# Between the states of a recurrence: pieces moved ahead of the last multiplications, experts' products weighted on ScalarE and added on GpSimd

## What is computed

```python
def _mamba_forward(x, W_in, conv_w, conv_b, W_xproj, W_dt, b_dt, A_log, D, W_out):
    u, z = jnp.split(x @ W_in.T, 2, axis=-1)
    uc = silu(conv3(u) + conv_b)            # depthwise, three taps over the sequence
    B_ssm, C_ssm, dt = split(uc @ W_xproj.T)
    delta = softplus(dt @ W_dt.T + b_dt)
    def step(h, inp):                       # over the 1024 positions, n = 16 states
        dA = jnp.exp(d_t[:, :, None] * A)
        h = dA * h + (d_t * u_t)[:, :, None] * b_t[:, None, :]
        y_t = jnp.einsum('bdn,bn->bd', h, c_t)
    return ((y + uc * D) * silu(z)) @ W_out.T

def _L0_ffn_ref(x, gate_w, W1, b1, W2, b2, sW1, sb1, sW2, sb2):
    combine = top-2 softmax weights, renormalised      # (tokens, 8)
    h = jax.nn.gelu(jnp.einsum('th,ehf->tef', x, W1) + b1)
    y = jnp.einsum('tef,efh->teh', h, W2) + b2
    return jnp.einsum('teh,te->th', y, combine) + gelu(x @ sW1 + sb1) @ sW2 + sb2
```

## Time and profile before

| | |
|---|---|
| median of 3 runs | 3067.3 us (3067.11 to 3069.73) |
| the profiled execution | 3073.01 us, of which the span of its instructions 3070.9 us |
| busy over the span | PE 78%, DVE 72%, ACT 55%, POOL 47% |
| loop of batch 0 | 72.8 to 270.6 us (197.8 us) |
| loop of batch 1, with the experts of batch 0 | 270.6 to 514.0 us (243.4 us) |
| loop of batch 2, with the experts of batch 1 | 514.0 to 766.7 us (252.7 us) |
| loop of batch 3, with the experts of batch 2 | 766.7 to 991.2 us (224.5 us) |
| experts of batch 3 | up products from 1031.3 us, last down product done 1158.4 us |
| the layers behind | the rest, to 3070.9 us |

### The profile page before, as it was taken

The page is one execution under the profiler, slowest core; times in us unless marked ns, Lnnn a source line. Parts: engine busy times, 40 slices in busy tenths (PEclk is TensorE's granted clock), DMA queues, the critical chain, the costliest instruction groups (busy, mean ns, idle before and its releaser), DMA issues.

```text
span 3070.9 us, 42340 instructions
## 1 busy us (share of the span) xinstructions
PE 2391.0 (78%) x15570; PEld 1711.5 (56%) x15570; DVE 2202.3 (72%) x3693; ACT 1696.2 (55%) x2621; POOL 1448.7 (47%) x1343
## 2 busy tenths in 40 slices
PE   2333579388488794999999999999999478767987
PEld 0101256156256572777677777777777356745675
DVE  5999999989986314888788878887888543354334
ACT  5333476376474342878777877787777224222322
POOL 0434323433433102655866676667567541564156
PEclk7555699698798896999999999999999789887988
DMA  3000000000000001101000000000000100000000
GB/s 103 0 0 0 1 1 1 0 1 1 0 1 1 1 1 40 26 24 29 21 23 22 22 22 22 22 22 21 22 22 1 42 1 1 1 14 1 1 1 14
DMA packets 32031, 42.04 MB, mean 14 GB/s; under 512 B 8897, under 2 KB 18130, under 8 KB 31442
## 3 DMA queue, kind: packets, MB, share of 16 engines
q1 hardware_dynamic: 31826, 39.34, 4.7%
HBM read 12.05 MB, written 2.10 MB: 5 GB/s over the span
## 4 chain that ended last, share of the span: by engine, by line
PE 49%; DVE 24%; issue 12%; POOL 9%; ACT 5%; SPq 1%; DMA 0%; POOLq 0%; DVEq 0%; ACTq 0%
PE ps L1073 10%; PE ps L1051 6%; PE ps L1062 6%; PE ps L828 5%; DVE MA L1209 3%; DVE lnb L315 2%; DVE BIG L340 2%; PE ps L757 2%; PE ps L1842 2%; PE ps L1033 2%; PE ps L759 2%; PE ps L758 2%; DVE BIG L334 2%; PE ps L1784 1%; DVE ps L328 1%
## 5 line engine op out<-in xcount | busy, mean ns | idle before, releaser
L1209 DVE TENSOR_REDUCE MA<-ps 128x1 f32<-128x1024 f32 x512 | 623.3, 1221 | 191.4 <-PE ps L1051 178.6
L423 POOL TENSOR_TENSOR MA<-MA,BIG 128x1024 f32<-128x1024 f32 x128 | 309.3, 2438 | 590.4 <-DVE BIG L340 559.1
L1073 PE MATMUL ps<-MA,WB 128*64 128x128 f32 x4096 | 504.4, 277 | 0.0
L1073 PEld LDWEIGHTS ps<-MA,WB 128*64 128x64 f32 x4096 | 442.6, 137 | 88.9 <-issue 87.9
L1051 PE MATMUL ps<-BIG 96*128 96x512 f16 x1024 | 313.8, 388 | 13.6 <-ACT WB L1136 5.0
L1136 ACT ACTIVATE WB<-ps,MA 128x1024 f32<-128x1024 f32 x206 | 229.7, 1115 | 149.2 <-DVE MA L1209 149.2
L828 PEld LDWEIGHTS ps<-WB,HR 128*128 128x128 f32 x2304 | 285.5, 199 | 32.5 <-issue 16.9
L828 PE MATMUL ps<-WB,HR 128*128 128x128 f32 x2304 | 295.5, 285 | 9.0 <-DVE acc L696 9.0
L744 ACT ACTIVATE HR<-ps,b 128x512 f32<-128x512 f32 x288 | 191.2, 687 | 174.1 <-PE ps L759 173.3
L1143 ACT ACTIVATE MA<-ps 128x1024 f32<-128x1024 f32 x256 | 259.9, 1015 | 5.0 <-PE ps L1062 5.0
L1605 POOL TENSOR_TENSOR BIG<-MA,BIG 128x512 f32<-128x512 f32 x128 | 132.2, 1049 | 232.3 <-PE ps L1828 74.5
(11 more groups left out here) (306 smaller groups left out, 5262.3 us busy)
## 6 DMA issues: line engine op xcount, KB each, us to landing
BIG<-BIG SPq DMA_DIRECT2D x192, 64.0 KB, 2.0
BIG<-WB SPq DMA_DIRECT2D x192, 64.0 KB, 2.0
WB<-w_dram SPq DMA_DIRECT2D x1, 2304.0 KB, 14.6
X<-x_dram SPq DMA_DIRECT2D x4, 512.0 KB, 12.5
HR<-w_dram SPq DMA_DIRECT2D x1, 2048.0 KB, 9.3
out_dram<-X SPq DMA_DIRECT2D x4, 512.0 KB, 3.2
WB<-wqkv_dram SPq DMA_DIRECT2D x1, 1536.0 KB, 6.3
WB<-w_dram SPq DMA_DIRECT2D x2, 512.0 KB, 8.3
```

The source lines that it names most:

```text
L423: e.tensor_tensor(yy[:, c, :], yy[:, c, :], db[n % 2][c], ALU.add).then_inc(*p_my.up(b, n, c))
L1073: x = e.matmul(bank[6][64 * pp:64 * pp + 64, 0:128], V[(4 * b + g) % 2][:, k, 64 * pp:64 * pp + 64], DT[n % 2][:, 128 * k:128 * k + 128], ...
L1209: e.tensor_reduce(L_of(n)[:, c:c + 1], ps[s][:, :], AX, ALU.max, negate=True).then_inc(*v_amx.up(n, s))
```

## The change

Five things change in the first two layers.

1. DVE's pieces are planned at 7.05 into a state's period, so that they stand between the scans and the multiplications at L340 (in the changed kernel L341). The period is 13 and a group of experts 8.6 (8.0 in the loop of batch 3); the other planned times follow.
2. The routed experts' down products of batches 0 to 2 are weighted by ACT (L776, four Identity activations of 128x128 with the routing weight as scale) into `weighted`, which is the memory of `lnp`, and added to acc by POOL (L727, 128x512). Each weighting waits for POOL's last addition; PE's next down product waits for the weighting. Batch 3 keeps DVE's instructions.
3. The first tap of the convolution, with its bias, is made by ACT (L470), both halves behind all four copies of u.
4. The rows of B and C are split in place, on the partitions that need it, without the two copies of 32 partitions.
5. `lnp`'s four loads leave the first constants and come behind the loads of the third layer; the fourth layer waits for them.

```diff
@@ -84,26 +84,29 @@
     return out
 
 
-N_PERIOD, M_PERIOD, M_FIRST = 14.0, 224.0, 56.0
+N_PERIOD, M_PERIOD, M_FIRST = 13.0, 208.0, 56.0
 PLAN = [(h, e) for h in range(2) for e in (8, 0, 1, 2, 3, 4, 5, 6, 7)]
 
 
-def slot(n, more=9.5):
+def slot(n, more=7.05):
     return N_PERIOD * n + more
 
 
-IN_AT0 = {"stats": 0, "norm": 5, "tr": 8, "u": 10, "conv0": 14.5, "conv1": 18, "silu": 21.8, "wx": 23.6, "bc1": 26.4,
+IN_AT0 = {"stats": 0, "norm": 5, "tr": 8, "u": 10, "tap0": 13, "tap1": 15, "conv0": 14.5, "conv1": 17.3, "silu": 21.8, "wx": 23.6, "bc1": 26.4,
           "bc2": 28.5, "wdt0": 28, "wdt1": 33.4, "exp": 36, "sp0": 39, "ln0": 41, "dl0": 43, "sp1": 45.6, "ln1": 47.6,
           "dl1": 49.6, "du": 52.2}
-IN_AT = {"stats": slot(4), "norm": slot(5), "tr": 82.5, "u": 87, "conv0": slot(6), "conv1": slot(7), "silu": 111.5,
-         "wx": 114.5, "bc1": slot(8), "bc2": slot(9), "wdt0": 119, "wdt1": 142, "exp": 146.5, "sp0": slot(10), "ln0": 153,
-         "dl0": slot(11), "sp1": slot(11, 12.2), "ln1": 169.5, "dl1": slot(12), "du": slot(15, 7.1)}
-OUT_AT = {"gate": slot(0), "yy": 12.2, "out": 12.5, "stats": slot(1), "rstd": 28.3, "norm": slot(2), "x": 42.3}
+IN_AT = {"stats": slot(4), "norm": slot(5), "tr": 75, "u": 79.5, "tap0": 84.7, "tap1": 88, "conv0": slot(6), "conv1": slot(7),
+         "silu": 101.5, "wx": 104.5, "bc1": slot(8), "bc2": slot(9), "wdt0": 109, "wdt1": 128, "exp": 133, "sp0": slot(10),
+         "ln0": 140.5, "dl0": slot(11), "sp1": slot(12), "ln1": 166.5, "dl1": slot(13), "du": slot(15)}
+OUT_AT = {"gate": slot(0), "yy": 9.8, "out": 10, "stats": slot(1), "rstd": 22.3, "norm": slot(2), "x": 35.3}
 OUT_AT3 = {"gate": 0.5, "yy": 0, "out": 3, "stats": 5.5, "rstd": 8.5, "norm": 10.5, "x": 13}
-F_AT = {"stats": 0, "norm": 14, "tr": 17, "flo": 24, "gate": 26.5, "top": 28, "e": 32, "wts": 35, "cT": 38, "k": 31,
-        "K": 9.0, "up": 0.9, "dn": 4.0, "dnj": 1.1, "done": 9.3, "end": 206, "rnorm": 213, "x": 216}
+F_FIRST = {"stats": 3, "norm": 7.5, "tr": 10.5, "flo": 14, "gate": 15.5, "top": 17.5, "e": 20.5, "wts": 23.5, "cT": 26.5,
+           "k": 18}
+F_STEP = {"K": 8.6, "up": 0.9, "dn": 4.0, "dnj": 1.1, "done": 8.7, "end": 182.3, "rnorm": 189.5, "x": 192.8}
+F_STEP2 = {"K": 8.0, "up": 0.8, "dn": 4.0, "dnj": 1.0, "done": 8.1, "end": 170.5, "rnorm": 176.5, "x": 179.8}
 F_AT3 = {"stats": 0, "norm": 5, "tr": 8, "flo": 9.6, "gate": 11, "top": 12.4, "e": 16, "wts": 17.4, "cT": 19.4, "k": 14.5,
          "K": 6.5, "up": 0.65, "dn": 2.7, "dnj": 0.9, "done": 6.8, "end": 142, "rnorm": 146, "x": 149}
+F_AT = [{**F_FIRST, **F_STEP}, {**F_FIRST, **F_STEP}, {**F_FIRST, **F_STEP2}, F_AT3]
 
 
 def l_at(b, n, more=0.0):
...
 def f_at(b, what, more=0.0, k=0):
-    f = F_AT if b < NB - 1 else F_AT3
-    return out_at(b, "x") + 4 + f[what] + more + (k * f["K"] if k else 0)
+    f = F_AT[b]
+    return out_at(b, "x") + 3.2 + f[what] + more + (k * f["K"] if k else 0)
 
 
...
         consts += [(wdt[96:104, :], d["wdt"]), (iota8[:, :], d["iota8"]), (tri[:, :], d["tri"]), (b2[:, :], d["b2"])]
-        for i in range(4):
-            consts += [(lnp[:, i, :], d["lnp"][i:i + 1, :].partition_broadcast(128)),
-                       (lam[:, i, :], d["lam"][i:i + 1, :].partition_broadcast(128))]
+        consts += [(lam[:, i, :], d["lam"][i:i + 1, :].partition_broadcast(128)) for i in range(4)]
...
             for c in range(2):
                 yield in_at(b, f"conv{c}")
-                e.wait_ge(*a_m.at("u", b, c, 1))
-                if c == b == 0:
-                    e.wait_ge(*p_const.at("pad"))
-                e.tensor_scalar(cv[c], u[:, c, 0:1024], cw[:, c, 0:1], cb[:, c:c + 1], ALU.mult, ALU.add).then_inc(
-                    *dve_own.up())
                 for k in (1, 2):
-                    e.wait_ge(*dve_own.now())
+                    if k == 1:
+                        e.wait_ge(*a_mtap.at(b, c))
+                    else:
+                        e.wait_ge(*dve_own.now())
                     i = e.scalar_tensor_tensor(out=cv[c], in0=u[:, c, k:k + 1024], scalar=cw[:, c, k:k + 1], in1=cv[c],
                                                op0=ALU.mult, op1=ALU.add)
                     i.then_inc(*(dve_own.up() if k == 1 else v_mconv.up(b, c)))
-            r, hi = projected[0:96, :], rows[b % 2]
+            r, hi = projected, rows[b % 2]
             yield in_at(b, "bc1")
             e.wait_ge(*a_m.at("wx", b, 1))
-            e.tensor_copy(bc[0], r).then_inc(*dve_own.up())
+            e.tensor_copy(hi, r[0:96, :]).then_inc(*dve_own.up())
             e.wait_ge(*dve_own.now())
-            e.tensor_tensor(r, r, bc[0], ALU.subtract).then_inc(*dve_own.up())
+            e.tensor_tensor(r[0:64, :], r[0:64, :], hi[0:64, :], ALU.subtract).then_inc(*dve_own.up())
             e.wait_ge(*dve_own.now())
             yield in_at(b, "bc2")
-            e.tensor_copy(bc[1], r).then_inc(*dve_own.up())
+            e.tensor_copy(hi[0:64, :], r[0:64, :]).then_inc(*dve_own.up())
             e.wait_ge(*dve_own.now())
-            e.tensor_tensor(hi, r, bc[1], ALU.subtract).then_inc(*dve_own.up())
-            e.wait_ge(*dve_own.now())
-            e.tensor_copy(hi[32:64, :], bc[1][32:64, :])
-            e.tensor_copy(hi[0:32, :], bc[0][0:32, :]).then_inc(*v_mbc.up(b))
+            e.tensor_tensor(hi[0:32, :], r[0:32, :], hi[0:32, :], ALU.subtract).then_inc(*v_mbc.up(b))
...
+            for c in range(2):
+                yield in_at(b, f"tap{c}")
+                for h in range(2):
+                    e.wait_ge(*a_m.at("u", b, c, h))
+                if c == b == 0:
+                    e.wait_ge(*p_const.at("pad"))
+                if c and b:
+                    e.wait_ge(*v_mdl.at(b - 1, 0))
+                e.activation(cv[c], up[b % 2][:, c, 0:1024], ACT.Identity, bias=small["convb"][:, c:c + 1],
+                             scale=small["convw"][:, c, 0:1]).then_inc(*a_mtap.up(b, c))
...
@@ -684,6 +692,8 @@
                 h, x = PLAN[kk]
                 if x == 8:
                     continue
+                if b < NB - 1:
+                    continue
                 yield done_at(b, kk)
                 e.wait_ge(*t_fdn.at(b, kk))
...
             rstd(e, st["f"]).then_inc(*p_frs.up(b, "in"))
+            for k in routed if b < NB - 1 else []:
+                yield done_at(b, k) + 1.4
+                h = PLAN[k][0]
+                e.wait_ge(*a_fcb.at(b, k))
+                if k > 1 and PLAN[k - 1][1] != 8:
+                    e.wait_ge(*p_fcb.at(b, k - 1))
+                e.tensor_tensor(acc[:, 4 * h:4 * h + 4, :], acc[:, 4 * h:4 * h + 4, :], weighted, ALU.add).then_inc(
+                    *p_fcb.up(b, k))
             yield f_at(b, "end", 2.5)
             e.wait_ge(*v_fst.at(b, "out"))
...
+                if k >= 1 and PLAN[k - 1][1] != 8 and b < NB - 1:
+                    yield done_at(b, k - 1)
+                    h, x = PLAN[k - 1]
+                    e.wait_ge(*t_fdn.at(b, k - 1))
+                    if k == 2:
+                        e.wait_ge(*v_fc.at(b))
+                    prev = [j for j in routed if j < k - 1][-1:]
+                    if prev:
+                        e.wait_ge(*p_fcb.at(b, prev[0]))
+                    elif b:
+                        e.wait_ge(*p_fcb.at(b - 1, 17))
+                    for j in range(4):
+                        i = e.activation(weighted[:, j, :], down(b, k - 1)[:, 128 * j:128 * j + 128], ACT.Identity, bias=0.0,
+                                         scale=G6[:, 4 * h + j, x:x + 1])
+                    i.then_inc(*a_fcb.up(b, k - 1))
                 if k >= 1 and PLAN[k - 1][1] == 8:
                     yield done_at(b, k - 1)
...
             e.dma_start(WB[:, 1536:2048], d["wout"].rearrange("p c n -> p (c n)")).then_inc(s_wa, 16)
+            for i in range(4):
+                e.dma_start(lnp[:, i, :], d["lnp"][i:i + 1, :].partition_broadcast(128)).then_inc(s_lnp, 16)
             for p in ORDER:
                 if p[0] == "op" and p[4] == 3:
...
                 e.wait_ge(*ready)
+                e.wait_ge(s_lnp, 64)
                 e.tensor_tensor(n1, n1, lnp[:, 2 * w - 2:2 * w - 1, :].to_broadcast([128, 8, 128]), ALU.mult).then_inc(
                     *dve_own.up())
```

19 lines of the change are left out of this document (11 added, 8 removed).

## The result

The changed kernel takes 3140.8 us (median of 4 runs, 3138.87 to 3147.30) against 3068.5 for the kernel before on the same chip: the ratio is 1.0236, 95% interval 1.0217 to 1.0255. It is 72 us slower. The forecast was 3088, slower by 20.5, and the range ended at 3140. The profiled execution spans 3136.8 us (before 3070.9), 65.9 more.

What follows compares the result with a forecast made beforehand. DVE was taken to bound loop 0, a ring of PE and ACT (up products, gelus) the loops of batches 1 and 2. Terms −0.5 − 19 + 27 + 22 − 9 = +20.5 on 3067.3 gave 3088 us; range 3005 to 3140.

Steps and rivals of the forecast that it cites:

- Loop 0: Batch 0's loop: moved pieces no longer meet POOL, −28; new wait for ACT's tap, +9; in all −19, to 179 us.
- The steps of the experts: Loop of batch 1, 15 steps from group 1 to 16: 171 plus 20 of waits, 191 us, 12.7 a step against 10.3.
- The 20 for the clock: In those steps, about six PE waits for a gelu that also lower the clock, 3.4 us each.
- Weighting ahead of the switch: Expert step where ACT weights before its table switch, so the trip waits for the down product: 12.1 us.
- switch ahead of the weighting: Expert step where ACT's table switch is done before the weighting: 7.75 + 1.35 = 9.1 us.
- Loop 1: Batch 1's loop: 75 before the steps, 191 in them, 4.5 behind: 270.5 against 243.4 us, +27.
- Loop 2: Batch 2's loop, by the same counting as batch 1's: 275 against 252.7 us, +22.
- Loop 3: Batch 3's loop and tail: group 16 at 214.5, batch 3's first up product at 255.5 instead of 264.6 us, −9.
- the 0 for POOL's 48 additions: POOL's additions to acc, 1.05 us each, fit its idle time: 0; if late, they would hold the down product.
- DVE as the bound: Rival, all four loops: ACT's weighting is hidden and DVE's work sets the time, 2913 us; chance 0.10.
- The worse ring: Rival, expert loops: POOL's additions queue behind the states' and delay weightings, clock low longer, +42, 3130 us; chance 0.15.
- The cheap weighting with a high clock: Rival, expert loops: weighting takes 1.1 us and waits don't lower the clock, 3027 us; chance 0.20.

Runs made afterwards that it cites:

- e12: The changed kernel with ACT's weighting planned 1.5 later in a group of experts (8.7 to 10.2): 3083.2 us.
- e1: The changed kernel with the weighting and its addition back on DVE for all batches: 3078.4 us.
- e3: The changed kernel with the weighting and the first tap both back on DVE: 3060.1 us.
- e5: The changed kernel with the tail of a batch's experts (statistics and norm of acc, POOL's sum) planned 13 later: 3127.7 us.
- e13: The changed kernel with the weighting planned 1.5 later, the experts' tail 13 later and the first tap on DVE: 3046.0 us.
- e6: The changed kernel without POOL's 48 additions and the waits for them, so routed experts of batches 0 to 2 miss from the output: 3117.9 us.
- e11: The changed kernel with each ACT weighting in eight pieces of 128x64 instead of four of 128x128: 3153.8 us.
- e10: Kernel before, DVE's pieces moved ahead of the multiplications by C in all four loops, splitting in place, later lnp load; old periods, weighting and taps on DVE: 3066.4 us.
- e9: e3 with DVE's pieces planned behind the multiplications by C again in the loops of batches 1 to 3: 3076.5 us.

## Why the prediction was wrong, step by step

The direction was right, and so was the mechanism in loops 0 and 1; the size was 3.5 times too small (72 against 20.5), and the time lay 0.8 us beyond the range. The profiled execution is 65.9 slower, 45.4 more than the sum. Two terms hold 38 of these: loop 2, where the first down product starts late, and loop 3, where it starts late too and POOL's additions, put at 0, lengthen the tail. Term by term:

- **Start**, −0.5: −0.9.
- **Loop 0**, −28 for the pieces and +9 for the wait, −19: −16.5. The pieces take the prices of the earlier trace rows, and the wait is 9.2, as forecast; that leaves 25.7 for the pieces.
- **The steps of the experts**, 171 and 20 for the clock, 191: 193.8 and 193.5. The granted clock in the steps was 0.85, as forecast. By the prediction's own count, from the down product of group 0 to that of group 15, they took 193.9 and 193.6. In loop 1 twelve of the fifteen came within 2 us of their forecast; the fifth, ninth and tenth took 19.7, 15.3 and 15.5 instead of 14.8, 12.3 and 8.5. The 20 for the clock weren't spread over the steps, so that the sum held may be luck in part. Weighting ahead of the switch and switch ahead of the weighting were put 3.0 us apart (12.1 and 9.1), 6.4 with the 3.4 for the clock; e12's average is 7. What did not hold is that the prediction laid the growth of the steps on the weighting, but for the broadcast in the step of 19.6: e1 shows that only 24 of the 44 us are the weighting's. The other 20 come with the new plan (20 and 14 when the tap is on DVE too, e3).
- **Loop 1**, +27: +32.8. The first down product came 77.0 into the loop instead of 75, the steps took 3 more than 191, and the next loop began 5.4 instead of 4.5 behind them.
- **Loop 2**, +22: +40.8. This is the first step that failed: the next loop "by the same counting, 275". With 191 and 4.5 that leaves 79.5 for the start, and the first down product comes 94.6 into the loop, 17.6 later than in loop 1. The kernel before showed such a difference already (103.9 and 93.9, 10.0 later), and the prediction carried loop 1's start over with 4.5 more. Batch 0's experts end 20.7 us into loop 2 (before: 25.5), but the change plans DVE's statistics of acc 12.8 into that loop, where the plan before had 28. The tables of times in the change said so, and the earlier trace rows that the last weightings come behind a loop's end; the prediction priced how long the steps last, and not which piece was planned ahead of their end. e5 wins 9 of the 17.6 back by planning the tail later, and in e13 the first down product comes at 80.9.
- **Loop 3**, −9: +10.6. The second step that failed, by 20. The first down product comes 92.0 into the loop, 15 later than in loop 1, and so the step to group 16 at 226.7 instead of 214.5, which is 12 of the 20. The tail from there to batch 3's first up product is 7 longer (48.6 against 41.2): POOL's last additions of the states wait in its queue behind those to acc. e6, without these, is 16.4 shorter from the start of loop 3 to batch 3, 6.2 of it by an earlier first down product. So the 0 for POOL's 48 additions was the wrong entry. The warning beside it had the wrong engine wait: late additions were to hold the weighting and PE's down product, but e6 leaves the steps as they were, and it was POOL's own next additions, and DVE's gate behind them, that waited.
- The experts of batch 3 and the layers behind, 0: −0.9 from the gate of batch 3 on (2026.4 against 2027.7 us from its first down product on).

Of the rivals, DVE as the bound did not occur. The worse ring (3130) was nearest in time, but its mechanism did not: e6 leaves the steps as they were. The cheap weighting with a high clock fell with e11 and e12: the weighting took 1.14 a group, as it wanted, and cost 62 all the same, by its wait and its place. Pieces that still meet POOL did not occur either: they took the prices of the earlier trace rows.

What stays open: by which waits the new plan alone makes the steps 14 to 20 us longer. The pieces' place and the periods each do it when changed alone (e10, e9), and together they don't add. Where the trips fall among the gelus differs between these orders, but a count of trips inside a group of gelus (16 before, 11 in e1 and e9, 18 in e10) doesn't follow the times, so a price for it isn't shown. Open too is how e12's 58 us divide between the weightings and the gelus that moved with them.

## What to carry to other kernels

An instruction moved to another engine takes its waits along. Before a product's way out of PSUM is handed to the engine that also feeds the producer, ask what stands behind it in that queue: here it cost 62 us in all (e1), and a planned time 1.5 later, which took eight weightings from ahead of a table switch and some gelus with them, won 58 of them back. When steps grow, also ask where the last of them ends, and what piece of the next stage was planned ahead of that point. And a gain proven in a stage with one bound (20 us in loop 0) can be taken there alone.

## What the runs showed of the hardware

POOL's addition of 128x512 was put at 1.05 us; here it took 1.27 by itself and 1.53 on average, and 3.22 at 1054.69 us, where it started 0.12 us behind a scan with both inputs in SBUF, which took its usual 2.26. The other way, one scan with both inputs in SBUF took 3.17 beside POOL (rows at 532.76 and 534.09 above), where the same scan elsewhere takes 2.27, and POOL's pair 6.65 instead of 4.66. This agrees with the lock on the shared port that the Trainium skill describes ("SBUF — State Buffer", Who interferes with whom). At 1054.69 it was the addition that lost time; in the rows at 532.76 both did, and the trace doesn't show by itself which held the other when. The table loads took 1283 ns each, and in e12 the gelu behind the load at 501.73 starts 1.30 after it: here too the drain that the Trainium skill adds ("ScalarE: Activation LUTs", What ACT_TABLE_LOAD costs) doesn't show. The clock behaved as in the earlier trace rows: after a wait of 4.68 us the first matmul of an up product took 0.61 us, after one of 1.94 us 0.39.
